# New places for the whole order, four buffers of squares in the first attention, and Newton steps of the layer norm in the PSUM bank

## The reference, cut to what matters

```python
def taylor_exp(x):
    x2 = (x[..., :, None] * x[..., None, :]).reshape(*x.shape[:-1], 256) / R2
    return jnp.concatenate([ones, x / RRD, x2 / RD], axis=-1)
A_qk = jnp.tril(jnp.einsum('bhnd,bhmd->bhnm', taylor_exp(q), taylor_exp(k)))
y = jnp.einsum('bhnm,bhme->bhne', A_qk, v)
y = y * rsqrt(mean(y * y) + 1e-5) * g_weight
out = y.transpose(0, 2, 1, 3).reshape(b, l, 1024) @ Wo.T
```

```python
for i in range(6):
    x = attn_layer(shift_tokens(x), Wqkv[i], q_scale[i], k_scale[i], Wo[i]) + x
    x = ffn_layer(shift_tokens(x), ln_g[i], ln_b[i], W1[i], b1[i], W2[i], b2[i]) + x
# ffn_layer: (x-mu)/sqrt(var+1e-5)*g+b, then a * gelu(gate) @ W2 + b2
```

## Time and profile before

| | us |
|---|---|
| median of 3 runs | 3311.55 (3308.06 to 3326.01) |
| the profiled execution | 3318.56 |
| its span | 3316.5 |
| PE busy | 3131.0 (94%) |
| VectorE busy | 2539.2 (77%) |
| ScalarE busy | 2541.5 (77%) |
| POOL busy | 2190.2 (66%) |

### The profile page before, as it was taken

How to read it: one execution, slowest core, us unless ns; L and a number is a source line. 1 busy time by engine, 2 the same in 40 slices (tenths; PEclk the granted TensorE clock), 3 DMA queues, 4 the chain that set the end, 5 groups by cost and what they waited for, 6 DMA issues and landing times.

```text
span 3316.5 us, 125574 instructions
## 1 busy us (share of the span) xinstructions
PE 3131.0 (94%) x52744; PEld 1984.5 (60%) x52744; DVE 2539.2 (77%) x3324; ACT 2541.5 (77%) x6058; POOL 2190.2 (66%) x1943
## 2 busy tenths in 40 slices
PE   6999997899999999999999999999999999999996
PEld 3444443666666666666666666666666666666663
DVE  3565665788888888887888787888888888788883
ACT  3666764678887888887888787878788888787884
POOL 0000002978788778788788877778888788877771
PEclk9999998899999999999999999999999999999998
DMA  3333232544454444444444444445544454544441
GB/s 96 78 79 79 75 79 64 170 147 146 155 158 156 145 151 145 161 153 152 139 156 152 157 146 150 140 159 159 157 144 157 138 163 150 163 136 150 149 137 31
DMA packets 253392, 449.40 MB, mean 136 GB/s; under 512 B 59678, under 2 KB 103964, under 8 KB 252700
## 3 DMA queue, kind: packets, MB, share of 16 engines
q1 hardware_dynamic: 226512, 424.86, 40.4%
q10 hardware_dynamic: 26316, 16.52, 1.8%
HBM read 124.21 MB, written 7.34 MB: 40 GB/s over the span
## 4 chain that ended last, share of the span: by engine, by line
PE 56%; DVE 11%; POOL 9%; ACT 8%; issue 7%; DMA 7%; SPq 3%; POOLq 0%; ACTq 0%; DVEq 0%
PE PS L555 55%; DMA TR<-TPB 5%; DVE TPB L949 3%; ACT SC L1249 2%; POOL K L1367 2%; POOL Q L1367 2%; POOL K L1349 2%; DVE MX L965 1%; ACT SX L1225 1%; SPq L522 1%; DMA root_scratch<-NV 1%; SPq L532 1%; DVE FX L819 1%; DVE H L817 1%; DVE PP L985 1%
## 5 line engine op out<-in xcount | busy, mean ns | idle before, releaser
L949 DVE SCALAR_TENSOR_TENSOR TPB<-PS,VEC,C 128x1024 f32<-128x1024 f32 x768 | 965.0, 1268 | 201.9 <-ACT SX L1225 153.2
L1249 ACT ACTIVATE SC<-PS,BQ,RQ 128x64 f32<-128x64 f32 x3072 | 957.1, 456 | 40.8 <-DVE BQ L971 40.6
L1225 ACT ACTIVATE SX<-PS 128x512 f32<-128x512 f32 x768 | 485.4, 632 | 226.8 <-PE PS L555 221.5
L1367 POOL TENSOR_TENSOR Q<-TPB,TR 128x512 f32<-128x512 f32 x384 | 495.6, 1291 | 86.9 <-DMA TR<-TPB 86.6
L1349 POOL TENSOR_TENSOR K<-K,RB 128x512 f32<-128x512 f32 x384 | 500.2, 1303 | 51.2 <-DMA RB<-root_scratch 50.5
L1367 POOL TENSOR_TENSOR K<-TPB,TR 128x512 f32<-128x512 f32 x384 | 496.8, 1294 | 0.0
L555 PE MATMUL PS<-LXH,LH 128*128 128x512 f32 x768 | 404.2, 526 | 25.6 <-DVE TPB L949 22.4
L1375 POOL TENSOR_TENSOR SC<-SC,RC 128x1024 f32<-128x1024 f32 x192 | 367.1, 1912 | 25.3 <-DVE RC L979 25.0
L555 PEld LDWEIGHTS PS<-PP,VV 64*64 64x64 f32 x12288 | 273.2, 133 | 160.5 <-issue 158.5
L555 PE MATMUL PS<-PP,VV 64*64 64x96 f32 (+1 forms) x12288 | 341.2, 246 | 29.5 <-DVE TPB L949 24.3
L555 PE MATMUL PS<-AOT,LO 128*128 128x512 f32 x768 | 355.9, 596 | 0.0
(11 more groups left out here) (167 smaller groups left out, 5729.7 us busy)
## 6 DMA issues: line engine op xcount, KB each, us to landing
TR<-TPB SPq DMA_DIRECT2D x768, 256.0 KB, 3.1
RB<-root_scratch SPq DMA_DIRECT2D x768, 128.0 KB, 3.5
PP<-PX SPq DMA_DIRECT2D x576, 64.0 KB, 2.3
PP<-PP SPq DMA_DIRECT2D x384, 64.0 KB, 2.0
PP<-PX SPq DMA_DIRECT2D x192, 60.0 KB, 2.0
WS<-in_wqkv ACTq DMA_DIRECT2D x72, 128.0 KB, 2.6
QA<-TH SPq DMA_DIRECT2D x128, 64.0 KB, 2.1
QA<-TL SPq DMA_DIRECT2D x128, 64.0 KB, 2.1
```

The costliest lines, as they stand in the source:

```text
L949: e.scalar_tensor_tensor(TPB[:, n % 3:4 + n % 2:3 + n % 2 - n % 3, w, :], g, VEC[:, l, 9 + w:10 + w], C[:, at:at + 1024].rearrange("p (o c ...
L1225: e.activation(SX[i % 4][:, :], bk("PJ", key)[:, :], ACT.Square).then_inc(sem["pj_act"], 1)
L1249: p = e.activation(SC[m % 2][:, g, :, :].rearrange("p x k -> p (x k)"), bk("S1", (m,), s)[:, at:at + 64], ACT.Exp, bias=BQ[m % 2][:, g:g + ...
L1367: e.tensor_tensor((Q, K)[w][:, n % 8, :], TPB[:, n % 3, w, :], TR[n % 2][:, w, :], ALU.add).then_inc(sem["ad_pool"], 1)
```

## The change

- Step t of the first attention takes offsets by t % 6 (`AS`, `ASa`, `ASd`, `AY`), a pair of heads by hp % 2 (`AG`, `AE`, `AEa`), and `AQ`, `AV`, `AM`, `AO` get one place for each of their stages of a batch.
- There are four buffers P; `ASa` of step t waits for `AY` of step t - 4 (t - 3 before).
- Even and odd slots of the layers have own places for `PJ`, `PQ`, `PT`, `TS`, `SS`, `AD`, `RB`, `PR`, `VP` and `VC`.
- `F2n` writes its first two Newton results to the PSUM bank in place of H[0]; the bank is held until the third.
- All numbers of `PLACE` are others.

```diff
@@ PLACE @@
-    "AS": -1.210, "ASa": -1.387, "ASd": -1.145, "AY": 0.834, ... "F2n": 14.912, "WO": (11.293, 11.685, 12.726, 13.181),
+    "AS": (-2.216, -0.676, -1.658, -0.854, -1.738, -1.250), "AY": (2.498, 1.699, 0.915, 0.785, 0.625, 0.070), ...
+    "F2n": 14.647, "WO": (6.852, 10.772, 12.616, 12.829), "VP": (-0.452, -0.638), "VC": (-0.611, -0.624),
@@ order @@
-                at(z + t + P[st], o.put, st, 24 * b + t)
+                at(z + t + P[st][t % 6], o.put, st, 24 * b + t)
-            lay(z + j + P["VP"], group, "VP", 8 * u + j, "vp_act", 8 * u + j + 1, P["VC"] - P["VP"])
+            h = j % 2
+            lay(z + j + P["VP"][h], group, "VP", 8 * u + j, "vp_act", 8 * u + j + 1, P["VC"][h] - P["VP"][h])
-        lay(z + P["F2"], group, "F2", u, "f2_dve", 3 * u + 1, P["F2n"] - P["F2"])
+        lay(z + P["F2"], group, "F2", u, "f2_dve", 3 * u + 3, P["F2n"] - P["F2"])
@@ build @@
+            P.append(sb("PA3", [128, 2, L], F32, ca))
@@ vector_program @@
-                    rsqrt(bk("F2", key)[:, :], H[0][:, :], FX[:, :], "f2_act", "f2_dve", u)
+                    v, x = bk("F2", key), FX[:, :]
+                    on.wait_ge("f2_act", 2 * u + 2)
+                    e.scalar_tensor_tensor(v, v, EPS, x, ALU.add, ALU.mult).then_inc(sem["f2_dve"], 1)
+                    on.wait_ge("f2_dve", 3 * u + 1)
+                    e.scalar_tensor_tensor(v, v, -0.5, x, ALU.mult, ALU.mult).then_inc(sem["f2_dve"], 1)
+                    on.wait_ge("f2_dve", 3 * u + 2)
+                    e.scalar_tensor_tensor(x, v, 1.5, x, ALU.add, ALU.mult).then_inc(sem["f2_dve"], 1)
@@ scalar_program, ASa @@
-                    if t > 2:
-                        on.wait_ge("ay_pe", t - 2)
+                    if t > 3:
+                        on.wait_ge("ay_pe", t - 3)
```

More of the change, by code:

```diff
@@ L29 @@
 PLACE = {
[12 rows of a table removed]
[9 rows of a table added]
+    "AQd": -0.460, "AV": (-12.499, -5.968, -5.211, 1.108, 2.460, 3.259, 5.266, 6.887), "AVa": -0.054,
[6 rows of a table added]
 }
@@ L186, in order @@
             for half in range(2):
-                t = z + 12 * half + P["AQ"][n]
+                t = z + P["AQ"][2 * half + n]
                 at(t, o.put, "AQ", b, half, n, banks=[(None, "aq_dve", 1, 1)])
@@ L191, in order @@
             for i in range(4):
-                t = z + 3 * i + P["AV"][n]
+                t = z + P["AV"][4 * n + i]
                 at(t, o.put, "AV", b, i, n, banks=[(None, "av_act", 1, 1)])
@@ L199, in order @@
             for st in ("AS", "ASa", "ASd", "AY"):
-                at(z + t + P[st], o.put, st, 24 * b + t)
+                at(z + t + P[st][t % 6], o.put, st, 24 * b + t)
         for hp in range(8):
[L202 to L205, removed]
+            for st in ("AG", "AE", "AEa"):
+                at(z + 3 * hp + P[st][hp % 2], o.put, st, b, hp)
+            t = z + P["AM"][hp]
             at(t, o.put, "AM", b, hp, banks=[(None, "am_dve", 1, 1)])
             at(t + P["AMd"], o.put, "AMd", b, hp)
-            at(z + P["AO"][0] + hp * P["AO"][1], o.put, "AO", b, hp)
+            at(z + P["AO"][hp], o.put, "AO", b, hp)
         norm("mid", b, z, P["NM"])
@@ L268, in order @@
         for j in range(8):
-            lay(z + j + P["VP"], group, "VP", 8 * u + j, "vp_act", 8 * u + j + 1, P["VC"] - P["VP"])
-            lay(z + j + P["VC"], o.put, "VC", 8 * u + j)
+            h = j % 2
+            lay(z + j + P["VP"][h], group, "VP", 8 * u + j, "vp_act", 8 * u + j + 1, P["VC"][h] - P["VP"][h])
+            lay(z + j + P["VC"][h], o.put, "VC", 8 * u + j)
         lay(z + P["WO"][0], group, "WO", u, "wo_dve", 2 * u + 2, P["WO"][3] - P["WO"][0])
@@ L285, in order @@
     for n in range(NS):
+        h = n % 2
         for w in range(2):
[L287 to L295, removed]
+            i, k = 2 * n + w, 2 * h + w
+            lay(n + P["PJ"][k], group, "PJ", i, "pj_dve", i + 1, P["PT"][k] - P["PJ"][k])
+            lay(n + P["PQ"][k], o.put, "PQ", i)
+            lay(n + P["PT"][k], o.put, "PT", i)
+            lay(n + P["SS"][h], o.put, "SS", i)
+            lay(n + P["AD"][h], o.put, "AD", i)
+        for st in ("TS", "RB", "PR"):
+            lay(n + P[st][h], o.put, st, n)
         if n % 4 == 0:
@@ L354, in build @@
             KA = sb("KA", [128, 6, L], F32R, ca)
-            sb("gap", [128, 2944], F32, ca)
+            P.append(sb("PA3", [128, 2, L], F32, ca))
+            sb("gap", [128, 1920], F32, ca)
             WOA = sb("WOA", [128, 8, 128], F32, ca)
@@ L647, in tensor_program @@
                             h = 2 * hp + s
-                            p = mm(yb[64 * s:64 * s + 64, 128 * j:512], V[:, j, 64 * h:64 * h + 64], P[t % 3][:, s, at:at + n],
+                            p = mm(yb[64 * s:64 * s + 64, 128 * j:512], V[:, j, 64 * h:64 * h + 64], P[t % 4][:, s, at:at + n],
                                    j == 0, j == 3)
@@ L882, in vector_program @@
                     if t % 3 < 2:
-                        d, x = P[t % 3][:, :, 0:128], 2
+                        d, x = P[t % 4][:, :, 0:128], 2
                     else:
-                        d, x = P[t % 3][:, :, :].rearrange("p s (x c) -> p (s x) c", c=256)[:, :, 0:128], 4
+                        d, x = P[t % 4][:, :, :].rearrange("p s (x c) -> p (s x) c", c=256)[:, :, 0:128], 4
                     tri = cn("tri").rearrange("p (o c) -> p o c", o=1).broadcast_to([128, x, 128])
```

2 lines of the change are left out of this document (1 added, 1 removed), and 27 rows, old and new, of the table PLACE.

## The result

| | before | after |
|---|---|---|
| median, us | 3312.04 (3308.06 to 3326.01) | 3226.88 (3217.46 to 3227.83) |
| profiled execution, its span, us | 3318.56, 3316.5 | 3217.46, 3215.7 |

The ratio is 0.9725, with an interval from 0.9703 to 0.9748: 85 us less, where the prediction said 39. A second set of runs of the same kernel (e13) gave 3224.72 (0.971, 0.9689 to 0.9732). The two profiled executions lie further apart than the medians, 101 us in place of 85: before's is 6.5 us over its median and after's 9.4 under.

What follows compares the result with a forecast made beforehand. The prediction took PE to bound the kernel. Gains of 23 (attention), 13 (Newton steps) and 3 (layer places) summed to 39 us off the profiled 3318.56, giving a median of 3272 us, range 3228 to 3310.

Steps and rivals of the forecast that it cites:

- What bounds the kernel: Whole program: PE sets the beat, busy 94% of the span; in the layers it waits 51.5 us for TPB.
- Term A: Attention: fewer changes of tile shape on PE, 543 to 309, save 27 us less 4: -23 us (0 to -47).
- The 4 us for new waits: Attention: paired AS fill both bank pairs and the next waits for ScalarE's squares; 4 us taken off the gain.
- about 58.5 us: Attention: sign to check, batches of about 58.5 us in place of 61.6, PE still busy above 98%.
- The count for the layers: Layers: 1538 changes of tile shape in both orders, so no gain from shapes there.
- Term B: Layers: Newton steps in the PSUM bank avoid slow reads of two SBUF tiles: -13 us (bounds 0 and 24.6).
- The bank is held longer, so this costs nothing: Layers: Newton bank held about 1.4 us longer, next user over 5 us behind; without that cover 67 us in all.
- Term C: Layers' new places: -17 us from spread output pieces, +14 us from closer bank reuse behind VP, net -3 us.
- the slow rival: End of a layer unit: S1 waits for VP's late copy, 1.4 us a unit, 67 us, total 3339; chance 0.10.
- the layers gain more: Layers' 51.5 us of TPB waits go almost whole and the attention gives 35: about 3235 us; chance 0.20.
- Pairs that starve PE: Attention: PE runs dry between pairs, its gain is lost, bank waits eat the layers' gain: 3305 us; chance 0.14.
- the Newton edit does nothing: Layers: the stall only moves, giving 3285 us, still faster; counted within the forecast's own 0.54 chance.

Runs made afterwards that it cites:

- e13: The changed kernel run again as it is, in a second set of runs: 3224.72 us, ratio 0.971.
- e1: The kernel before with only the new attention order and four buffers, old layer places, Newton steps in SBUF: 3288.14 us, ratio 0.9928.
- e9: The changed kernel with two of six AS places moved so stages part again, 434 shape changes in place of 309: 3242.39 us, ratio 0.976.
- e5: The changed kernel with three buffers of squares in place of four, same order: 3219.51 us, ratio 0.9728.
- e6: The kernel before with four buffers of squares and all its old places: 3313.06 us, ratio 1.0006.
- e2: The kernel before with only the layers' new places, old attention, Newton steps in SBUF: 3317.91 us, ratio 1.0007.
- e3: The kernel before with only the first two Newton results written to the PSUM bank, all old places: 3307.89 us, ratio 0.997.
- e4: The changed kernel with its Newton steps back in SBUF, all places as changed: 3273.28 us, ratio 0.9882.
- e7: The changed kernel with the second Newton step writing SBUF, so the third reads two SBUF tiles: 3235.48 us, ratio 0.9774.
- e8: The changed kernel with all four output projection pieces (WO) at their old places: 3202.73 us, ratio 0.9679.
- e10: The changed kernel with only the first output piece moved, from 6.852 to 10.75, next to the second: 3209.66 us, ratio 0.9665.
- e11: The changed kernel with old output piece places, third Newton result left in the bank, held until F3: 3232.91 us, ratio 0.9734.

## Why the prediction was right and wrong

**What bounds the kernel** held. PE is the beat in both blocks, and in the layers 36 of the 51.5 us went in which it waited for a bank of TPB.

**Term A, right mechanism, too small.** 43 us (e1: 41) for a predicted 27 less 4. The change of shape was priced at 0.12 and 0.10 us, and measured at 0.154 to 0.17 (e9), above the price of both large parts. PE in the attention of after, 176 to 180 us, two stages `AS` joined (512 and 384 columns, listed together) and then three `AY`:

```profile
176.23 0.67 PE L560 MATMUL PS<-QA,KA 64*128 64x512 f32 x4
176.84 2.37 PE L560 MATMUL PS<-PA,VA 128*64 128x512 f32 x16
179.14 0.50 PE L560 MATMUL PS<-R,bselr 128*128 128x512 f32 x1
```

And before, where they stand apart:

```profile
183.07 0.44 PE L555 MATMUL PS<-QA,KA 64*128 64x384 f32 x2
183.45 0.87 PE L555 MATMUL PS<-PA,VA 128*64 128x256 f32 x8
184.25 0.50 PE L555 MATMUL PS<-R,bselr 128*128 128x512 f32 x1
...
189.35 0.87 PE L555 MATMUL PS<-PA,VA 128*64 128x384 f32 x4
190.15 1.12 PE L555 MATMUL PS<-AO,WOA 128*128 128x512 f32 x2
```

The two `AS` take 0.61 us together (176.23 to 176.84) and took 0.43 and 0.38 apart: 0.20 for one join. The sixteen products take 2.30 us and took 1.01, 0.80 and 0.80: 0.31 for two joins. The rows had allowed just these two values, 0.20 as the bound and 0.16 as the most; I chose below both, for `AS` because a third of them are narrow, for `AY` because an end is modelled, though the trace of before has starts on either side. The 4 us for new waits were not there: from 163.8 to 444.9 us PE waits 0.6 us for PA. So the fourth buffer, to which I gave a share in that, had nothing to do (e5, e6). Of the check I gave, "about 58.5 us", it was 56.0 to 57.5. The count for the layers was wrong: PE's matmuls between the first and the last rotation change their tile shape 1624 times before and 1584 times after. By e9's price the 40 are an estimated 6 us that the sum put at nothing; e2 has the same 1584 and shows no gain.

**Term B is the step that failed**, 13 us where the edit was worth 46 to 57. The steps themselves behave as predicted. The instructions of after's second and third step (minimum, median, maximum):

```profile
L1008 DVE SCALAR_TENSOR_TENSOR PS<-PS,FX x48: 699/700/700, 636.7 to 3183.8; 128x512 f32<-128x512 f32 x48
L1010 DVE SCALAR_TENSOR_TENSOR FX<-PS,FX x48: 691/691/692, 637.4 to 3184.6; 128x512 f32<-128x512 f32 x48
```

No spread is left, and writing the bank costs 8 ns at the most. For the places before, the 13 us were good too (e3: 10.9 between the rotations, 10 by the ratio). But I worked the price out from before's rows, and added it to another term that moves the same steps ahead of both rotations. There the edit is worth 57 us between the rotations, 46 by the medians. The bound "24.6, the whole excess" had the same fault: the excess itself is 43 us there (e4), and a lump of 1.5 us can stop PE where spread lateness would not. I had shown in the order of VectorE that both rotations now stand behind the steps, and drew nothing from it for the sum.

The rule named in the prediction, from the Trainium skill's page "SBUF — State Buffer", SBUF: two separate sides, agrees with e7: one step that reads two SBUF tiles, beside POOL's work, went from 691 to 1012 ns on the mean and to 1781 at most, with the median at 693.

**"The bank is held longer, so this costs nothing"** was right for the kernel as predicted: after lists no wait for FX. It holds for that order alone. With the first output piece late, PE waits for just this bank 38 to 40 times, 12.8 us (e8) and 14.7 us (e10). Held until `F3` (e11), the plan passes it over, and the waits are 67 us, as much as I had put on the lost cover; the program lost 18 to 32 of them.

**Term C, a net of -3, was +2 (e2), but for other reasons.** (1) I gave the spread of the output pieces 17 us of gain, for "the first of them ahead of the last `PV`". It costs 11 to 17 us between the rotations (e10, e8): I priced what PE does meanwhile, and not that a bank is away from the ring for it, which is the likely cause. (2) The waits for VV, 14 us, were 2.1 us as far as they are listed, 7 times, 0.3 at the longest. That is also the end of the slow rival, the late copy at a unit's end: it needed more than 1.2 us in each of 48 units.

**The sum** failed since it was a sum. The rival "the layers gain more" (3235) named both sizes nearly: 35 from the attention and the 51.5 us for TPB. Its mechanism was only half right: 36 of these 51.5 went, and over half of the gain lies in no listed wait. "Pairs that starve PE" fell with e1, "the Newton edit does nothing" with e3 and e4.

What stays open: the 8 us that e1's old layers lost; how the layers' gain divides between the steps' slowness, their place and the free banks, which work together, and a full cross of them wasn't run; and whether e8 and e10 gain by the bank or by the place of the piece's matmuls.

**A version better than both** is the change with a first output piece that doesn't hold a bank for six slots: e8 and e10, 3203 to 3210 us, ratios 0.968 and 0.967.

## What to carry to other kernels

Price an edit in the order in which it will run, not in the one that the trace shows: ask what stands behind the slow step there, and how many buffers of the ring are free at that time. A stage that is issued in pieces holds its bank from the first piece to the last; price that hold too, and not only what the engine does meanwhile. A wait that goes can come back under another name, so judge by the program's time and not by the row that shrank. Where ends are modelled, read a saving from starts on both sides, and don't take the sum of listed waits for all that better places can give.

## What the runs showed of the hardware that was not expected

**The granted clock falls behind the smallest matmuls, in some batches.** Once a batch PE makes 16 matmuls of 4 or 8 columns (`CX`), 1.9 us together, with no listed idle time around them. In after, the mean granted clock of the 4 us behind them is 0.57 to 0.64 in four of seven batches, which is mostly the lower level of 1.2 GHz, and 1.00 in three. Before, it is 1.00 in six of seven, one at 0.68. Neither PE's busy time nor the kind of its work differs. One window after such a fall:

```profile
215.70:219.70 4.00, 4.00 (x17) 1.18 (x16) 2.52 (x7) 1.09 (x2) 0.00 (x0) 0.57 0.43 107
```

The same group of PE behind `CX` in after, at the low clock and in the next batch but one at the full clock:

```profile
216.88 1.94 PE L560 MATMUL PS<-sq,C 128*32 128x512 f32 x8
...
331.58 1.06 PE L560 MATMUL PS<-sq,C 128*32 128x512 f32 x8
```

Such a batch takes 57.5 us and the other 56.0, so each fall costs 1.5 us, and three more of them took some 4.5 us off the attention's gain, an estimate. In e1 it falls in four of seven too (0.57 to 0.66). But this doesn't go with the new order alone. e3 has the attention of before word for word, and the clock falls in four of its seven later batches (0.57 to 0.71), and e5, with the new order, has two. One of e3's windows:

```profile
171.20:175.20 4.00, 4.00 (x17) 1.58 (x18) 3.11 (x6) 1.30 (x2) 0.00 (x0) 0.57 0.33 82
```

Which batches it falls in, and why, is open.

**Other VectorE work got slower with the new places.** By form, after:

```profile
L976 DVE SCALAR_TENSOR_TENSOR BQ<-MX,RQ 128x16 f32<-128x16 f32 x187 | 107.2, 573 | 6.5
...
L1015 DVE TENSOR_TENSOR H<-H,FX 128x512 f32<-128x512 f32 x48 | 43.5, 907 | 0.2
```

Before, these two took 455 and 679 ns. Both read two SBUF tiles. In e4, with the same places, they take 657 and 848, in e2 663 and 904, and in e3, with the old places, 446 and 681, so this comes with the places. In e2 VectorE is some 50 us busier for it (2117.9 us in place of 2063.9, from 700 to 3200), which may be why new places alone gained nothing. The excess of the small one, 16 columns wide, is 22 us on VectorE ((573 - 455) x 187), nearly the 24.6 that the two Newton steps had before. Whether it reaches PE wasn't tried.
